# Attention heads of a decoder layer: the second copy of the queries moves to VectorE, the scores for the maxima come one block later, and the PSUM banks are dealt out anew

## What is computed

```python
sel = jnp.argmax(gates, axis=-1)
gm = jax.nn.one_hot(sel, EXPERTS, dtype=x.dtype) * gates
values = jnp.einsum('bhne,ehdk,bnd->bhnk', gm, value_experts, x)
sim = jnp.einsum('bhid,bhjd->bhij', q * SCALE, k)
sim = jnp.where(causal_mask, jnp.finfo(sim.dtype).min, sim)
attn = jax.nn.softmax(sim, axis=-1)
out = jnp.einsum('bhij,bhjk->bhik', attn, values)
out = jnp.einsum('bhne,ehkd,bhnk->bhnd', gm, output_experts, out)
```

## Time and profile before

| | us |
|---|---|
| median of 3 runs | 982.74 (978.9 to 983.92) |
| the profiled execution | 980.29 |
| its span, first to last instruction | 978.5 |
| mean granted clock of TensorE | 0.986 of full |
| heads, batch 0 | about 252 to 407 of the span |
| heads, batch 1 | about 730 to 882 of the span |

### The profile page before, as it was taken

How to read it: one execution, slowest core, us unless ns; L and a number is a source line. 1 busy time by engine, 2 the same in 40 slices (tenths; PEclk the granted TensorE clock), 3 DMA queues, 4 the chain that set the end, 5 groups by cost and what they waited for, 6 DMA issues and landing times. The chain is left out here.

```text
span 978.5 us, 15283 instructions
## 1 busy us (share of the span) xinstructions
PE 924.8 (95%) x5740; PEld 706.4 (72%) x5740; DVE 648.4 (66%) x1022; ACT 358.4 (37%) x644; POOL 405.0 (41%) x363
## 2 busy tenths in 40 slices
PE   5979999999999898999999998999999999899998
PEld 3568778887656555589975886888876556549998
DVE  3857566547664647689869675755575564749887
ACT  3634555120366555301124355620105454631000
POOL 5312412212797868748630032400035665774100
PEclk9999999999999999999999999999999999999999
DMA  6104000434244550377540000022222010123763
GB/s 212 38 14 129 2 1 1 146 120 140 77 152 140 167 158 17 100 188 206 183 141 0 2 1 1 2 91 89 81 76 49 12 35 12 44 71 111 216 190 105
DMA packets 52463, 86.07 MB, mean 88 GB/s; under 512 B 11127, under 2 KB 32343, under 8 KB 52391
## 3 DMA queue, kind: packets, MB, share of 16 engines
q1 hardware_dynamic: 51111, 80.91, 27.0%
q10 hardware_dynamic: 1280, 4.20, 1.9%
HBM read 61.39 MB, written 19.33 MB: 82 GB/s over the span
## 5 line engine op out<-in xcount | busy, mean ns | idle before, releaser
L1099 DVE TENSOR_REDUCE region<-ps 128x1 f32<-128x512 f32 (+1 forms) x192 | 97.3, 550 | 77.4 <-PE ps L1471 76.4
L1143 DVE COPY_PREDICATED region<-region,ps 128x512 f32<-128x512 uint32 x112 | 82.0, 736 | 72.0 <-PE ps L1228 71.4
L1571 PE MATMUL ps<-expert_hi,kst 128*128 128x256 f32 x512 | 124.7, 283 | 3.6 <-DVE kst L1172 3.4
L1571 PE MATMUL ps<-expert_lo,kst 128*128 128x256 f32 x512 | 123.2, 279 | 0.0
L633 POOL TENSOR_TENSOR xT<-xT,region 128x896 f32<-128x896 f32 (+2 forms) x48 | 84.2, 1755 | 60.6 <-PE ps L1494 35.6
L1228 PE MATMUL ps<-expert_hi,wide_hi 128*128 128x512 f32 x256 | 102.7, 401 | 0.0
L1571 PEld LDWEIGHTS ps<-expert_hi,kst 128*128 128x128 f32 x512 | 96.2, 188 | 6.6 <-issue 6.6
L1228 PE MATMUL ps<-expert_hi,wide_lo 128*128 128x512 f32 x256 | 100.1, 391 | 0.0
L1228 PE MATMUL ps<-expert_lo,wide_hi 128*128 128x512 f32 x256 | 99.8, 390 | 0.0
L1172 DVE TENSOR_TENSOR kst<-region 128x1024 fp32r<-128x1024 f32 x64 | 82.1, 1282 | 23.0 <-PE ps L1577 14.7
L1571 PEld LDWEIGHTS ps<-expert_lo,kst 128*128 128x128 f32 x512 | 96.3, 188 | 0.0
(11 more groups left out here) (160 smaller groups left out, 1946.0 us busy)
## 6 DMA issues: line engine op xcount, KB each, us to landing
region<-hot_rows SPq DMA_DIRECT2D x128, 128.0 KB, 3.2
halves_kept<-expert_hi SPq DMA_DIRECT2D x16, 512.0 KB, 5.4
halves_kept<-expert_lo SPq DMA_DIRECT2D x16, 512.0 KB, 6.1
expert_hi<-halves_kept SPq DMA_DIRECT2D x64, 128.0 KB, 2.9
expert_lo<-halves_kept SPq DMA_DIRECT2D x64, 128.0 KB, 3.1
expert<-in_value_experts SPq DMA_DIRECT2D x8, 512.0 KB, 4.4
kx<-kst ACTq DMA_DIRECT2D x16, 256.0 KB, 2.9
expert<-in_output_experts SPq DMA_DIRECT2D x8, 512.0 KB, 4.4
```

Of the source, the lines that this page charges most:

```text
L1099: dve.tensor_reduce(mx[:, i, at_mx:at_mx + 1], ps[:, max_bank(h, m), 0:w], AX.X, ALU.max).then_inc(sem["s_max"], 1)
L1143: dve.copy_predicated(V3_heads[:, t], chosen.unsqueeze(3).broadcast_to([P, PAIRS3, 2, HD3]), ps[:, n % 4, :].rearrange("p (a i k) -> p a i ...
L1571: mm(ps[:, 4 + t // 2, t % 2 * D:(t % 2 + 1) * D], kst[n % 2][:, t * P:(t + 1) * P], w[:, slot, columns], start=(n == 0 and t % 2 == 0 and ...
```

## The change

DVE's `split` makes the second copy of the queries between its two key instructions, and ACT's `queries_twice` is gone. The scores of the next head begin after block 4 instead of 3 and the transpose of the maxima comes after block 10 instead of 9. Key tile 2 is weighed at block 11 with tiles 3 and 4. The scores for maxima have two banks, the transposed scores three (4, 5, 2). On DVE `factors` comes after the maxima instead of before, and `weighted` comes in the middle of the maxima of heads 5 and 7 instead of after those of heads 4 and 6; the last four come later among the output experts. The sums of head 6 are multiplied at block 9 of head 7 instead of block 6. In batch 0 SP takes the first denominators and factors after later pieces.

```diff
             qk_ps=PAIRS3 * 2 * NC, qk_sb=PAIRS3 * 2 * NC,
-            qq_ready=2 * H3, kst_ready=2 * H3, qx_ready=H3, o_sb=2 * H3, den_ps=H3, den_sb=H3, summed=H3 * (TT - 1),
+            qq_ready=H3, qq_twice=H3, kst_ready=2 * H3, qx_ready=H3, o_sb=2 * H3, den_ps=H3, den_sb=H3, summed=H3 * (TT - 1),
             factors_ready=PAIRS3, o_round=PAIRS3 * NC, o_lo_ready=PAIRS3 * NC,
...
         SPLIT_AT = {(0, 3): 0, (0, 8): 1, (1, 3): 2, (1, 8): 3, (2, 3): 4, (3, 3): 5, (3, 8): 6, (4, 3): 7}
-        ROUND_AT = {(5, 4): 0, (5, 6): 1, (6, 4): 2, (6, 6): 3}
-        ROUND_LATE_AT = {3: 4, 5: 5, 13: 6, 15: 7}
+        ROUND_AT = {(5, 4): 0, (5, 6): 1, (7, 1): 2, (7, 2): 3}
+        WEIGHTED_AFTER = 6
+        ROUND_LATE_AT = {6: 4, 7: 5, 14: 6, 16: 7}
         PARTS = [(p, c * CH, (c + 1) * CH) for p in range(PAIRS3) for c in range(NC)]
-        FACTORS_LATE_AT, WEIGHTED_LATE_AT = 4, (8, 9)
+        FACTORS_LATE_AT, WEIGHTED_LATE_AT = 6, {3: 4, 4: 5, 11: 6, 12: 7}
         SUMS_LATE_AT = 1
...
         SCORES = [(t, c) for t in range(TT) for c in range(t // TC + 1)]
-        SCORES_AT = {3: (0, 1, 2), 4: (3, 4), 5: (5, 6), 6: (7, 8), 7: (9, 10), 8: (11,)}
-        MAX_ROW_AT = 9
+        SCORES_AT = {4: (0, 1, 2), 5: (3, 4), 6: (5, 6), 7: (7, 8), 8: (9, 10), 9: (11,)}
+        MAX_ROW_AT = 10
         PROJECT_AT = (3, 5, 7, 11)
...
         SUM_BANK = (7, 3)
-        WEIGH_AT = {6: (0, 1), 9: (2,), 11: (3, 4)}
-        LATE_AT, LATE, SUMS_AT = 1, (5, 6, 7), 6
+        WEIGH_AT = {6: (0, 1), 11: (2, 3, 4)}
+        LATE_AT, LATE = 1, (5, 6, 7)
+        sums_at = lambda h: 6 if h < H3 - 1 else 9
         OUT_AT, DEN_AT = 3, 8
-        MAX_BANKS = 3
-        max_bank = lambda h, m: ((4, 5, 7) if h == 0 else (0, 1, 2))[m % MAX_BANKS]
+        MAX_BANKS = 2
+        max_bank = lambda h, m: ((4, 5) if h == 0 else (0, 1))[m % MAX_BANKS]
+        ST_BANKS = (4, 5, 2)
+        st_bank = lambda g: ST_BANKS[g % len(ST_BANKS)]
         PROJECT_FIRST, SCORES_FIRST = 4 * TT, 5 * TT + 4
...
                     turn_gates(0)
-                if q == E3 + SPLIT_AT[3, 3]:
+                if q == E3 + SPLIT_AT[3, 8]:
                     keep_den(0, 0)
...
                     turn_den(0, 0)
+                if q == E3 + SPLIT_AT[4, 3]:
                     spread_factors(0, 0)
...
                             until(sp, "kst_ready", b, 2 * H3)
-                            until(sp, "qq_ready", b, 2 * H3)
+                            until(sp, "qq_ready", b, H3)
+                            until(sp, "qq_twice", b, H3)
                             until(sp, "qx_ready", b, H3)
...
                 i, own = h % 2, HALF * (h % 2)
-                until(pool, "qq_ready", b, 2 * h + 1)
+                until(pool, "qq_ready", b, h + 1)
                 if h >= 2:
...
                         until(act, "qx_ready", b, 2 * p)
-                        until(act, "qq_ready", b, 4 * p)
+                        until(act, "qq_twice", b, 2 * p)
                     act.activation(raw[:, i, c * CH:(c + 1) * CH], ps[:, 6, :], ACT.Copy,
...
                     copy(qq[i][own:own + HALF, :], raw[own:own + HALF, 0, :], "qq_ready")
-
-                def queries_twice(h):
-
-                    i, own, oth = h % 2, HALF * (h % 2), HALF * (1 - h % 2)
-                    copy(qq[i][oth:oth + HALF, :], raw[own:own + HALF, 0, :], "qq_ready")
                 def keys_twice(h):
...
                         queries_high(0)
-                        queries_twice(0)
                         keys_twice(0)
...
                             until(act, "summed", b, (h - 1) * (TT - 1) + j)
-                        act.activation(kept(b, h, j)[:, q0 - j * P:q1 - j * P], ps[:, 4 + g % 2, 0:q1 - q0], ACT.Exp
+                        act.activation(kept(b, h, j)[:, q0 - j * P:q1 - j * P], ps[:, st_bank(g), 0:q1 - q0], ACT.Exp
                                        ).then_inc(sem["pt_ready"], 1)
...
                         if h + 1 < H3 and n == 1:
-                            queries_twice(h + 1)
-                        if h + 1 < H3 and n == 2:
                             keys_twice(h + 1)
...
                             output_copy(h - 1, n - OUT_AT)
-                        if h and n == DEN_AT:
+                        if h and n == max(DEN_AT, sums_at(h)):
                             den_copy(h - 1)
...
                                     ).then_inc(sem["kst_ready"], 1)
+                    dve.tensor_copy(qq[i][oth:oth + HALF, :], raw[own:own + HALF, 0, :]
+                                    ).then_inc(sem["qq_twice"], 1)
                     until(dve, "kst_ready", b, 2 * h + 1)
...
                     split(h)
+                    for m in range(NB):
+                        maximum(h, m)
+                        if m == WEIGHTED_AFTER and h >= 5 and h % 2:
+                            weighted(h - 5)
+                            weighted(h - 4)
+                    max_row(h)
                     if h >= 4 and h % 2 == 0:
                         factors(h // 2 - 2)
-                    for m in range(NB):
-                        maximum(h, m)
-                    max_row(h)
-                    if h >= 4 and h % 2 == 0:
-                        weighted(h - 4)
-                        weighted(h - 3)
                 factors(PAIRS3 - 2)
...
                     masked(n)
-                    if n < 2:
-                        weighted(H3 - 4 + n)
                     if n == FACTORS_LATE_AT:
...
                     if n in WEIGHTED_LATE_AT:
-                        weighted(H3 - 2 + WEIGHTED_LATE_AT.index(n))
+                        weighted(WEIGHTED_LATE_AT[n])
                     if b + 1 < B and n in STATS_AT:
...
                     if m == 0:
-                        until(pe, "qq_ready", b, 2 * h + 2)
+                        until(pe, "qq_ready", b, h + 1)
+                        until(pe, "qq_twice", b, h + 1)
                         until(pe, "kst_ready", b, 2 * h + 2)
...
                         w = q1 - q0
-                        until(pe, "pt_ready", b, g - 1)
-                        bank, key, query = 4 + g % 2, slice(key_tile * P, (key_tile + 1) * P), slice(q0, q1)
+                        until(pe, "pt_ready", b, g + 1 - len(ST_BANKS))
+                        if h == 0 and n == ST_BANKS.index(2):
+                            until(pe, "val_v", b, TT * (E3 - 1))
+                        bank, key, query = st_bank(g), slice(key_tile * P, (key_tile + 1) * P), slice(q0, q1)
                         mm(ps[:, bank, 0:w], kst[i][:, key], qq[i][:, query], start=True, stop=False)
...
                                 weigh(h - 1, j)
-                        if n == SUMS_AT and h:
+                        if n == sums_at(h) and h:
                             denominators(h - 1)
```

## The result

The changed kernel takes 987.37 us at the median of 17 runs (982.06 to 993.91), the kernel before 981.37 at the median of 17 beside it. The ratio is 1.0074, with a 95% interval of 1.0055 to 1.0092: slower by 6 to 7 us. The profiled execution took 990.36 us with a span of 988.6, which is 10.1 more than the span before. In the changed kernel the lines of the code have moved by a few: plain scores are L1467 (mask L1470), their transpose L1478, weighing L1493, sums L1503, transposed scores L1541, 1542 and 1544, DVE's maxima L1099, its short reduction L1103, its split L1083 (keys), L1085 (the new query copy) and L1088 (subtraction), POOL's `queries_low` L524, its sums L639.

The account below looks back on a forecast made before the run. PE was taken as the bound, busy 924.8 of 978.5 us. Gains -30.4, costs +41.4 and clock -3.4 gave +7.6 on 980.3, or 990.3 on the median 982.7, stated as 990.0; own range 984 to 997, 8 in 10 971 to 1000.

Parts of the forecast that it names:

- (a): Transposed scores in the heads: with three banks, ten waits for ACT should go, gaining 5.4 us.
- (b): Transposed scores: two more bank waits for ACT, 3.2 us together, should go, gaining 4.0 with another of 0.35.
- (c): Sums of head 6: needed later, so PE's waits for POOL should all go, gaining 4.0 us.
- (d): First scores of heads: the old waits in 14 places should go, gaining 11.8 us.
- (e): Weighing on PE: one visit less in each of 16 heads, gaining 3.2 us, between 0 and 4.3.
- (f): Output experts: more items between `weighted`, `factors` and SP's fetches, gaining 2.0 of 3.4 us, between 0 and 3.
- (h): DVE's split of three, taking turns with POOL: first scores wait, costing 11.9 us, between 1 and 17.
- (i): Two banks for maxima: scores 2 and 8 wait for earlier maxima, costing net 5.9 us over 14 heads.
- (j): Transpose of the maxima: PE stands 0.8 us for DVE's short reduction in 14 heads, costing 11.2.
- (k): `weighted` between the maxima of heads 5 and 7: scores 9 wait, costing 12.4 us, between 2 and 15.6.
- (l): TensorE's clock in the heads: six old falls go, four new come, net -3.4 us, between -10.2 and +3.
- DVE wins the turns: Rival: POOL does not hold DVE, so split costs 5 and `weighted` 4; 972 us, chance 0.22.

Follow-up runs that it names:

- the third experiment: Changed kernel with DVE's two weighted products moved behind the row of maxima of heads 5 and 7: 979.06 us, ratio 0.9980 to the kernel before.

## Why the prediction came out right, and where its steps were off

The time forecast was 990.0, slower by 7.6 on its own execution; it came out as 987.4, slower by 6 to 7. The mechanism was the forecast's: old waits cured, new ones for DVE in their place. The size was in part luck: the forecast had +11.0 from waits and visits and -3.4 from the clock, the account has +4.8, and +2 on the mean of all executions (+4.8 in the profiled pair). Step by step, against the account above:

- **(a), (b)** 9.4 expected, 8.1 by the waits. Two of 0.2 are left. But the experiment with the banks as before shows that in head 0 the gain only lengthened the wait for the split. The prediction priced that wait as it would stand with the third bank, so the sum holds; read alone, the term (a) promised a gain which the bank could not give while the split was late.
- **(c)** 4.0 expected, 4.2 came; alone, on the kernel before, it gives 7.8 with what the clock gives back.
- **(d), (e), (f)** The 11.8 of (d) went as counted. The 3.2 of (e) is taken over into the account; the kernel with one visit more gives 4.7, with an interval of 1.5 to 8. (f) gave 1.5 for 2.0.
- **(h)** 11.9 expected, 9.2 by the waits. Head 0, the largest part, came as expected, 2.7 for 2.81 and 2.72 shown, by the turns that the prediction wrote out. Head 6 was priced a little high (1.7, for 1.21 + 0.17), head 4 waited once, for 0.39, and head 2 and head 1 of batch 0 did not wait. The overtaking in head 1 of batch 0 came when tile 2 was moved behind block 10 (2.89), and with the banks as before (2.17), once each.
- **(i)** 5.9 expected, 4.6 measured: 0.38 at each of 12 scores 2, as priced, and nothing at scores 8.
- **(j)** 11.2 expected, 10.5 measured, called the surest and it was. The mask to the short reduction's end took 1.16, in the changed kernel as before.
- **(k)** 12.4 expected, 7.0 measured, the term that was most mis-sized. The prediction took the middle between "DVE first by 0.05" and "POOL first". DVE was first all four times, by 0.07 to 0.09, and the pair then took 2.9, not 3.1. The step that failed first is the middle itself, 3.2 of the 5.4 too much: a race with a known order of issue has two outcomes, and the rows had DVE ahead. The other 2.2 is in the waits for that outcome, 1.6 and 3.0 in the prediction, 1.1 and 2.4 (with the 0.17) in the trace.
- **(l)** the clock was the one term with the wrong sign: -3.4 expected, +4.8 found in the profiled pair and about +2 on the mean of all executions. The prediction counted four new falls of 3.4 us, 1.7 lost in each. The profiled execution has as much time at 1.2 GHz as nine: behind each wait of head 0 two in a row, and more in heads 6 and 7 of both batches. That some of it was luck is seen in the third experiment, which has the same waits in head 0 and one fall in each.
- **Not foreseen:** 2.3 us at projections in batch 0. `queries_low` starts right behind POOL's own sums, ACT may not overwrite `raw` before it has been read, and PE waits for ACT's bank. The waits are there too with the query copy on ScalarE (2.0) and with the banks as before (1.7), so neither part makes them; a likely reason is that PE has two blocks of scores fewer in front of the same projection, which no run shows by itself. One of the two:

```profile
296.79 2.37 POOL L524 TENSOR_TENSOR qx<-region,qq 64x1024 fp32r<-64x1024 f32 x1
...
299.32 0.60 ACT L816 ACTIVATE region<-ps 128x512 f32<-128x512 f32 x1 [2.21 <-POOL qx L524]
...
299.97 0.50 PE L1450 MATMUL ps<-wide_hi,W_hi 128*128 128x512 f32 x1 [1.19 <-ACT region L816]
```

The four costs came out 10.1 lower than priced (31.3 for 41.4), 2.3 came unforeseen, the gains were 1.6 smaller, and the clock was 8.2 dearer: -10.1 + 2.3 + 1.6 + 8.2 = +2.0, so the sum was closer than its terms. That is luck: costs priced too high stood against a clock with the wrong sign. Of the rivals, "DVE wins the turns" fell in the first trace (the split of head 0 took 5.4, from 734.75 to 740.19, where that rival wanted 3), though DVE's being first in each race made (k) cheap; the third bank did what it says; short waits did not hold the clock down: between 747 and 847 there are the waits of five heads at scores 2 and at the transpose, each below 1 us, and the clock is at 1.00. The Trainium skill's case of micro-idles at rotating banks (TensorE: Matmul & The Clock Gate, A second HAM failure mode: psum-queue depth-cycling) is therefore not what this kernel met. The Trainium skill's rule on the shared port, that whoever issues first has it for the whole instruction (SBUF — State Buffer, Who interferes with whom), agrees with the two timelines of the subtraction, 3.38 and 1.22.

## What to carry to other kernels

Where two engines take turns at a port, price an operation by what the other has issued just before it; one more short instruction in a chain is one more chance for the other's long one to get in, and either holding that one back or moving the short one elsewhere cures it. Where a bound engine waits in several places of a row, a gain ahead of a late step can be given back there, as in head 0, where the third bank's 1.5 us only lengthened the wait for the split; so judge a part of a change with its neighbours in place. And count the clock with each wait, over many executions: the two waits of 2.7 to 2.8 us in head 0 were each followed by a loss of 3.4 us in the profiled execution.

## What the runs showed of the hardware beyond the expected

The length of a wait alone doesn't say whether TensorE's clock falls behind it. It stayed at 2.4 GHz behind 1.20 us in head 0 of the kernel with the banks as before; in the changed kernel it fell behind 1.21 at 858.55, for about 3.4 us, and stayed at 1.00 behind the same 1.21 at 377.55, for the 8.5 us until 386. The fall (windows: stretch and length, PE busy, granted clock, DMA share, GB/s):

```profile
858.50:859.50 1.00, 0.74 (x5) 1.00 0.64 178
859.50:860.50 1.00, 1.00 (x4) 0.55 0.01 2
...
863.50:864.50 1.00, 1.00 (x8) 1.00 0.00 0
```

A long wait need not bring a fall either. In the kernel with tile 2 behind block 10, head 0 of batch 1 has the wait of the changed kernel, and the clock is at 1.00 in the window around it and in the next, until 767:

```profile
742.01 0.30 PE L1467 MATMUL ps<-kst,qq 128*128 128x128 f32 x1 [2.71 <-DVE kst L1088]
...
727.00:747.00 20.00, 17.15 (x83) 1.00 0.34 98
```

Nor does it say for how long. Behind the two waits of 2.7 and 2.8 in head 0 the changed kernel was at 1.2 GHz for 6.8 us each time; with the same waits, the kernel with the pair behind the row of maxima shows half of that in windows around the same place, 20 x 0.09 = 1.8 us lost in each, for 20 x 0.17 = 3.4 there. The changed kernel's windows:

```profile
255.90:262.70 6.80, 6.51 (x22) 0.53 0.50 141
740.20:747.00 6.80, 6.55 (x20) 0.50 0.10 19
```

And windows of 20 us of the kernel with the pair behind the row of maxima:

```profile
250.00:270.00 20.00, 16.33 (x78) 0.91 0.34 95
727.00:747.00 20.00, 17.00 (x77) 0.91 0.25 68
```

The executions spread accordingly: 982.1 to 993.9 in 17 of the changed kernel, whose clocks go from 0.976 to 0.990. What decides between the cases, no run here shows.
